# Attention's side work in another order: o at step 9, q at 11, k and V at 13

## The reference

```python
x = x + 0.5 * ffn(_layernorm(x))
x = x + attn(_layernorm(x))     # 16 heads of 8, softmax over 256 keys, biases, output projection
x = x + 0.5 * ffn(_layernorm(x))

def attn(x):
    q, k, v = proj(Wq, bq), proj(Wk, bk), proj(Wv, bv)
    scores = einsum('bhqd,bhkd->bhqk', q, k) * 8 ** -0.5
    o = einsum('bhqk,bhkd->bhqd', softmax(scores), v)
    return o.reshape(B, S, E) @ Wo.T + bo
```

## Time and profile before

| | |
|---|---|
| time, median of 3 runs | 623.62 us (618.94 to 626.49) |
| the profiled execution, its own time | 617.05 us |
| its span in the profile | 615.2 us |
| mean granted clock of PE | 0.99 |
| PE busy | 589.1 us, 96% |
| PEld busy | 439.3 us, 71% |
| DVE busy | 443.6 us, 72% |
| ACT busy | 466.4 us, 76% |
| POOL busy | 98.3 us, 16% |

### The profile page before, as it was taken

The page is one execution under the profiler, slowest core; times in us unless marked ns, Lnnn a source line. Parts: engine busy times, 40 slices in busy tenths (PEclk is TensorE's granted clock), DMA queues, the critical chain, the costliest instruction groups (busy, mean ns, idle before and its releaser), DMA issues.

```text
span 615.2 us, 12580 instructions
## 1 busy us (share of the span) xinstructions
PE 589.1 (96%) x4452; PEld 439.3 (71%) x4452; DVE 443.6 (72%) x1000; ACT 466.4 (76%) x796; POOL 98.3 (16%) x262
## 2 busy tenths in 40 slices
PE   2999999999999999999999999999989999999996
PEld 2788788788686766565656565766678878788785
DVE  7995855868558778798988897885665756855742
ACT  4677977968865578788787878877877977968964
POOL 2092020022021103132231302102020020020000
PEclk9999999999999799999999999999999999999999
DMA  8300000000074306171625343400000001000011
GB/s 282 86 2 1 0 2 1 0 0 1 1 273 145 130 2 220 56 255 62 235 89 187 137 139 142 134 2 1 2 1 1 1 1 36 0 26 8 1 34 37
DMA packets 36693, 42.02 MB, mean 68 GB/s; under 512 B 2464, under 2 KB 27296, under 8 KB 36640
## 3 DMA queue, kind: packets, MB, share of 16 engines
q1 hardware_dynamic: 36640, 41.31, 19.8%
HBM read 22.42 MB, written 18.87 MB: 67 GB/s over the span
## 4 chain that ended last, share of the span: by engine, by line
PE 73%; ACT 9%; DVE 8%; issue 5%; DMA 3%; SPq 1%; POOL 0%; ACTq 0%; DVEq 0%; POOLq 0%
PE bank L1092 39%; PE bank L1204 9%; PE bank L1179 8%; PE bank L1191 4%; PE bank L1193 3%; DVE silu L842 3%; DVE act_lo L833 2%; ACT silu L544 2%; DVE neg_max L883 2%; PE bank L1161 1%; PE bank L1222 1%; PE bank L1169 1%; ACT act_hi L536 1%; ACT act_hi L559 1%; DMA QK<-qk_scratch 1%
## 5 line engine op out<-in xcount | busy, mean ns | idle before, releaser
L1092 PE MATMUL bank<-act_hi,WH 128*128 128x512 f32 x576 | 230.5, 400 | 3.8 <-ACT act_hi L559 1.5
L1092 PE MATMUL bank<-act_lo,WH 128*128 128x512 f32 x576 | 225.7, 392 | 0.0
L883 DVE TENSOR_REDUCE neg_max<-bank 128x2 f32<-128x512 f32 x256 | 166.8, 681 | 32.6 <-PE bank L1179 30.4
L678 ACT ACTIVATE probs<-bank 128x512 f32<-128x512 f32 x256 | 139.3, 598 | 38.6 <-PE bank L1193 37.0
L853 DVE TENSOR_TENSOR act_lo<-full,act_hi 128x512 fp32r<-128x512 f32 x128 | 91.5, 719 | 101.7 <-ACT act_hi L559 101.4
L557 ACT ACTIVATE full<-bank,SG 128x512 f32<-128x512 f32 x128 | 88.1, 688 | 65.8 <-PE bank L1092 65.0
L1092 PEld LDWEIGHTS bank<-act_hi,WH 128*128 128x128 f32 x576 | 108.2, 188 | 31.2 <-ACT act_hi L559 4.7
L1092 PEld LDWEIGHTS bank<-act_lo,WH 128*128 128x128 f32 x576 | 108.3, 188 | 23.1 <-issue 1.0
L1191 PE MATMUL bank<-QK 32*128 32x256 f32 x512 | 96.1, 334 | 0.4 <-ACT probs L678 0.4
L559 ACT ACTIVATE act_hi<-bank,SG 128x512 fp32r<-128x512 f32 x128 | 87.1, 681 | 0.0
L1193 PE MATMUL bank<-m_parts,SEL 32*128 32x256 f32 x512 | 82.1, 280 | 0.0
(11 more groups left out here) (94 smaller groups left out, 570.7 us busy)
## 6 DMA issues: line engine op xcount, KB each, us to landing
qk_scratch<-qk SPq DMA_DIRECT2D x64, 256.0 KB, 2.6
QK<-qk_scratch SPq DMA_DIRECT2D x16, 1024.0 KB, 7.6
raw_rest<-w_ffn SPq DMA_DIRECT2D x4, 512.0 KB, 5.8
out<-X SPq DMA_DIRECT2D x4, 512.0 KB, 3.2
X<-x SPq DMA_DIRECT2D x3, 512.0 KB, 7.7
raw<-w_ffn SPq DMA_DIRECT2D x3, 256.0 KB, 4.5
X<-x SPq DMA_DIRECT2D x2, 256.0 KB, 3.2
WA<-w_att SPq DMA_DIRECT2D x1, 256.0 KB, 5.6
```

The lines of the kernel that those rows point to most:

```text
L678: A.activation(probs[:, v % 8, :], bank[B_BANKS[bb][v]][:, :], ACT.Exp, scale=SCALE)\
L883: D.tensor_reduce(neg_max[:, bb, qt, n0:n0 + 2], bank[(banks or A_BANKS[bb])[u]][:, :].rearrange("p (h k) -> p h k", h=2), axis=AX.X, op=A ...
L1092: ins = MM(dst, a, b, start=k == 0, stop=k == len(todo) - 1)
```

## The change

It changes at which steps the side work runs, the waits that go with the new order in bank 6, and the order of GpSimd's queue. No arithmetic is added or removed. `tokens_of_o` moves from step 13 to 9 in every call, with its readers on DVE from 14 and 15 to 10 and 11. V moves from 9 to 13 in the even calls; q from 9 to 11 and k from 11 to 13 in the odd ones, ACT's copies with them. V and q now wait for `o_norm` of the same call; the row maxima wait for `k_full` or `v_set`. DVE's normalisations go to 8, 9, 12, 13, and its statistics to 4, 7, 8, 9, 12, 13. On GpSimd the low part of q goes between the two doublings, that of k behind them, ahead of the 1/sqrt steps.

```diff
-TOKENS = 13
+TOKENS = 9
@@ GpSimd
-            def max_again(b, bb):
+            def max_again(b, bb, q=None):
                 for qt in range(2):
+                    if q is not None and qt == 1:
+                        low_part(q, 0)
                     pool.wait_ge(max_done, UNITS * b + 8 * qt + 8)
...
+                if q is not None:
+                    low_part(q, 1)
...
-            low_parts(2)
             pool.wait_ge(bias_set, 1)
             with pool.Fori(1, NPAIR - 2) as i:
-                max_again(2 * i, 0)
+                max_again(2 * i, 0, i + 1)
                 norm_for(i)
                 add_bias(2 * i - 2)
                 max_again(2 * i + 1, 1)
                 add_bias(2 * i - 1)
-                low_parts(i + 2)
-            max_again(NBATCH - 4, 0)
+            max_again(NBATCH - 4, 0, NPAIR - 1)
@@ ScalarE, attend
-                    if u == (9 if prev else 5) and v_pair is not None:
+                    if u == (13 if prev else 5) and v_pair is not None:
                         set_v(*v_pair)
...
-                    if u in (9, 11) and ahead is not None:
-                        full_part(ahead, (u - 9) // 2)
-                    if u in (10, 12) and ahead is not None:
-                        high_part(ahead, (u - 10) // 2)
+                    if u in (11, 13) and ahead is not None:
+                        full_part(ahead, (u - 11) // 2)
+                    if u in (12, 14) and ahead is not None:
+                        high_part(ahead, (u - 12) // 2)
@@ VectorE, att_body
                     even = {u: lambda t=t: normalise(n, tile0 + t, t, 1, last=t == 3)
-                            for t, u in enumerate((8, 9, 10, 11))}
+                            for t, u in enumerate((8, 9, 12, 13))}
...
-                    odd = dict(zip((4, 5, 7, 8, 9, 11), norm_steps(norm_of(q), 4 * q, 4, halves=True)))
+                    odd = dict(zip((4, 7, 8, 9, 12, 13), norm_steps(norm_of(q), 4 * q, 4, halves=True)))
...
-                    odd[10] = lambda: normalise(NORMS1, 0, 0)
-                    odd[11] = lambda: normalise(NORMS1, 4, 4)
+                    odd[12] = lambda: normalise(NORMS1, 0, 0)
+                    odd[13] = lambda: normalise(NORMS1, 4, 4)
@@ TensorE, attend
                     if prev2:
                         pe.wait_ge(o_norm, b - 1)
-                    elif prev:
-                        pe.wait_ge(v_set, pair + 2)
+                    if pair + 1 < NPAIR:
+                        if bb == 0:
+                            pe.wait_ge(k_full, pair + 1)
+                        else:
+                            pe.wait_ge(v_set, pair + 2)
                     max_rows(b, bb)
...
-                    if u == (9 if prev else 5) and v_pair is not None:
-
-                        if prev2:
-                            pe.wait_ge(att_added, b - 1)
+                    if u == (13 if prev else 5) and v_pair is not None:
+
+                        if prev:
+                            pe.wait_ge(o_norm, b)
                         pe.wait_ge(m_lo, b + 1)
                         project_v(v_pair, 6)
...
-                    if u == 9 and ahead is not None:
-                        project_q(ahead, 6)
-                    if u == 11 and ahead is not None:
-                        pe.wait_ge(q_full, ahead)
-                        project_k(ahead, 6)
                     if u == TOKENS and own and prev:
 
                         if ahead is not None:
-                            pe.wait_ge(k_full, ahead)
-                        elif v_pair is not None:
-                            pe.wait_ge(v_set, v_pair + 1)
+                            pe.wait_ge(a_xT_sb, ahead + 1)
                         elif prev2:
                             pe.wait_ge(att_added, b - 1)
                         tokens_of_o(b - 1)
+                    if u == 11 and ahead is not None:
+                        pe.wait_ge(o_norm, b)
+                        project_q(ahead, 6)
+                    if u == 13 and ahead is not None:
+                        pe.wait_ge(q_full, ahead)
+                        project_k(ahead, 6)
```

## The result

The changed kernel takes 636.26 us in the median (632.04 to 643.34), the kernel before, run beside it, 621.34 us (618.76 to 626.49): 1.025 times as long, interval 1.019 to 1.031, so slower; between the medians lie 14.9 us. The ratio leaves out the slowest of the six executions (643.34), which counts as one of a slower state; without it the changed kernel's median is 633.96. The profiled execution took 638.56 us, with a span of 636.2 and a mean granted clock of 0.97 (before: 617.05, 615.2, 0.99).

The account below looks back on a forecast made before the run. TensorE was taken to bound attention, so only waits count: odd calls 4.5, even calls 1.3, loads 3.7, together +9.5 us. On the runs' median of 623.62 that gave 633.1, written 633, range 622 to 638.

Parts of the forecast that it names:

- What bounds the kernel: In attention TensorE (PE) is busy nearly throughout; moving full-size pieces frees nothing, so only waits that come or go count.
- The wait that goes: Odd calls of pairs 1 to 4: x transposes at step 7 stop waiting for DVE's addition to X, -1.6 us.
- `o_norm` ahead of q: Odd calls, step 11: q waits 0.86 us for DVE's in-order queue to scale o; odd calls 4.5 us in all.
- not slower: Rival: norm_o and scale_o run in DVE's gaps, q meets no wait, only -1.6 stays, 622 us; chance 0.18.
- Pair 0, 1.06: Pair 0's odd call has no addition ahead, so it gains nothing there and grows by the full 1.06 us.
- k, 0.24: Odd calls: k waits for ACT's copy of q (`q_full`), 0.24 us more of stall.
- pair 5, 0.76: Pair 5's odd call has no statistics, so DVE's chain is shorter and the call grows by 0.76 us.
- V, 0.25 in five calls: Even calls: V at step 13 waits 0.25 us for `o_norm` in pairs 1 to 5; 1.3 us with pair 6.
- GpSimd's order: Earlier doublings bring nothing, k's later low part does not decide its writes, and the swap's cost is covered.
- The loads: k's writes on SP start 2.0 us later, Q and K loads lose 1.75 of slack; stalls 3.7 us together.
- worse: Rival: every load is late as pair 2's, 7 us or more for loads, 637 us and up; chance 0.12.
- 1.75 earlier: Rival that loads stay hidden, 629.4 us: needs loads landing 1.75 us sooner than pair 3's did; chance 0.2.

Follow-up runs that it names:

- e1: Kernel before with only DVE's statistics moved to steps 4, 7, 8, 9, 12, 13; 619.21 us, ratio 0.999.
- e8: Changed kernel with the statistics' aggregation and variance at steps 12 and 13, half and guess at 14 and 15; 632.71 us, ratio 1.020 to the kernel before.
- e6: Changed kernel with the first load of pairs 2 to 7 issued ahead of that pair's writes, reading old scratch content; 626.54 us, ratio 1.009 to before.
- e14: Kernel before with only the even calls' new order: o at 9, V at 13, normalisations at 8, 9, 12, 13; 622.21 us, ratio 1.003.
- e2: Kernel before with only GpSimd's order changed: q's low part between the doublings, k's behind them; 624.00 us, ratio 1.0048.
- e5: Changed kernel with GpSimd's queue in its old order, both low parts and then the doublings; 633.67 us, ratio 1.020 to the kernel before.
- e7: Changed kernel with SP writing q's high part, then its low part, then k's likewise, each when ready; 625.27 us, ratio 1.0066 to the kernel before.
- e13: The changed kernel once more, unedited, for another profile; 638.12 us, ratio 1.023 to the kernel before.
- e12: Kernel before with two of one pair's writes repeated by SP and awaited ahead of its load; 625.74 us, ratio 1.011.
- e9: Kernel before with statistics at 4, 7, 8, 9, 12, 13 and SP writing high parts first; 619.10 us, ratio 0.9969.
- e11: Kernel before with six of one pair's writes repeated by SP and awaited ahead of its load; 627.23 us, ratio 1.011.
- e3: Changed kernel with V, o and the even calls' normalisations back in their old places; 638.36 us, ratio 1.032 to the kernel before.

## Why the prediction was right, and where it was not

633 was forecast, in a range of 622 to 638, with slower as the likeliest; 636.26 was measured. The distance to before, 14.9 us between the medians, is larger than the 9.5 of the sum, so the steps have to be judged one by one. It was luck in part that the total came so close: the base was set 2.3 too high, which hid some of what the sum lacked.

- **What bounds the kernel.** Right. PE's start-to-start times carried over to a hundredth: a pair, `weigh` and a transpose cost in after what they cost in the earlier trace rows.
- **The wait that goes.** Right: 0.39 forecast, 0.38 in e1.
- **`o_norm` ahead of q.** Right, and the main step. It names L906 in six odd calls, q starts at t + 4.03, and the odd calls are 15.92 to 16.09 in pairs 1 to 4 where the clock is full, and 15.80 in pair 5. The sum of DVE's steps in order gave it. The rival "not slower" rested on DVE being ahead on average; its busy share is hardly over 80% in both kernels, and it was the order that decided. e8 shows how little room that order has: work moved behind q came back as a wait elsewhere.
- **Pair 0, 1.06; k, 0.24; pair 5, 0.76; V, 0.25 in five calls.** Right: 0.97 (e6), 0.17 to 0.2 beside k's name, 0.77, and 13.63 against 13.36 in e14 (pair 1's 0.35 apart).
- **GpSimd's order.** Half right. That it brings nothing holds in the old order (e2), and that k's low part doesn't set k's writes holds in after, where SP's eight writes run on without a gap; k's begin 2.2 us into the even call, as forecast, in five of six calls (3.9 in the one of the timeline above). But the text weighed it only there and at nothing: in the old order the swap costs about 2.7 us, and in the new order it saves some 7 us of waits for the doublings and brings as much in load waits (e5). It was argued from a trace in which k starts at t + 3.5 (316.55, behind `weigh`), 2.5 us earlier than after the change.
- **The loads.** The mechanism is right: SP's queue is late, L1181 waits for the load in five calls, and e6 and e7 remove it. The term is mis-sized: 3.7 forecast, 6.8 in after's profile, 5.8 in e13's (6.3 of waits less pair 2's).

  Pair by pair, forecast and after's profile: pair 2, 1.7 more than before, and its old 0.5 was gone; pair 3, 0.9 and 0.91; pair 5 (the timeline's), none and 1.14; pairs 4, 6 and 7, 0.35 each and 2.76, 0.90 and 1.62. So the delay of SP's queue was right, and the slack that it was set against was wrong. The rival "worse" had 7 for this term and came nearer, but not for its reason: it took every load to be as late as pair 2's, and pair 2's was not late at all.

  The slack was taken from single landings (6.0) and from four writes of 2.49 us as if these were fixed. In after's profile the five loads that are waited for took 5.9 to 7.2 us to land. The last write ahead of them took 3.2 to 4.6 us from issue to landing; in before 2.6 to 2.9 for pairs 5 to 7, but 4.0 and 4.5 for pairs 4 and 3. Against before, pair 4 lost 1.5 us in the issue of its writes, one of which took 2.28, and 1.3 on the load's landing; pair 5 lost 1.5 on the last write's landing, out of a slack of 2.4. Pair 2, which was to be the surest stall, gained 1.4 on the last write's landing and 1.4 on the load's. Whether the later order of q and k itself makes the landings longer is not shown. The "1.75 earlier" that a load would have needed to stay hidden is about the scatter of the DMAs themselves. The estimate of 4.4 us by the fit in the page "DMA: Bandwidth & Descriptors" of the Trainium skill (the anatomy of one DMA) is under all that were measured. That section of the Trainium skill gives its fit for DMAs issued by GpSimd, which the prediction did not say; these are issued by SP.

SP's issues of L353, after and then before: least, median and most, in ns.

```profile
L353 SPq DMA_DIRECT2D qk_scratch<-qk x64: 518/609/2280, 168.7 to 401.4; - x64
```

```profile
L353 SPq DMA_DIRECT2D qk_scratch<-qk x64: 517/606/630, 168.2 to 380.0; - x64
```

The clock line of before's page, for the next point:

```profile
PEclk9999999999999799999999999999999999999999
```

- **The clock.** Missing. No term of the sum, no rival and no part of the range had it, though before's page already shows the lower clock once, at attention's entry. It has two shares. The one in the middle belongs to the change, through the load waits, as far as the profiles show (it came in five of the seven with load waits of 0.8 us and more, and in none of the seven others): 4.1 us in after's profile, 5.7 in e13's. The one at the entry does not: it lasted 10.2 us in the profiles of before, e6, e8 and e12, 13.7 in e7, 17.1 in e1, 20.5 in after, e2, e5, e9, e11, e13 and e14, and 23.9 in e3, whatever the kernel was. Ten us more of it cost 3.6 us (the first two calls of attention in e2 against before). It is also one reason why executions of the same kernel lie apart. Among after's six the mean clock goes with the time: 0.987 at 632.04 us, 0.964 at 643.34. At the same mean clock the two kernels lie closer than their medians: at 0.984, 632.44 us against 619.9 to 622.4 for before; at 0.99, 631.68 (e13) against 617.7 to 618.8. That is 10 to 14 us, about the 12 of order and load waits.
- **The base.** The forecast was set on a median of 623.62; beside the changed kernel the one before had 621.34. So the forecast of 633 is closer in absolute time than its sum: that was 5.4 us short, and the base 2.3 us high.

Put together: order 5.7 (forecast 5.8), loads 6 to 7 (3.7), clock in the middle 4 to 6 (0). That is 16.6 in the profiled execution of after and 17.2 in that of e13, against 14.9 between the medians. So in the medians some 3 us are left for the clock; how much of it stands in the middle and how much at the entry is not on record there.

## What to carry to other kernels

When side work is moved, add up the in-order queue of each reader from the instruction that releases it; here that gave waits right to 0.02 us, while busy shares said nothing. Treat a DMA's landing and issue as a spread, not as one number: here a load with a slack of 2.4 us, delayed by 1.75, was not in time but waited for, for 1.14 us. The cheap cure was to issue what is ready first. And look at the granted clock in every stretch before and after: a short wait on TensorE's path can cost more in the call behind it than it lasted.

## What the hardware showed that was not expected

- The lower clock behind a wait doesn't scale with it: 0.81 us was followed by 2.84 us of loss, 5.3 by 2.0, 3.2 by 4.3, and 1.9 by none (e13, e11, e12, e13).
- The issue of one write on SP took at most 0.63 us in before and e1, 2.28 in after, 1.6 to 1.7 in e3, e6 and e7, for writes of the same size; 1.5 in e12 and 1.9 in e9 show that it does not take the new order of q and k. Its cause was not tried.
- The landings of the first 1 MB load of a pair lie between 5.9 and 7.2 us within one execution of after, and between 5.9 and 7.4 in before.
